# DRAM-to-DRAM copies in a selective scan: ScalarE's queue issues them in place of SyncE's

## The chip, the cores and the metric

One core of a Trainium2 chip. The metric is the device time of one execution in microseconds (us), lower is better. A core has TensorE (PE), VectorE (DVE), ScalarE (ACT), GpSimd (POOL) and SyncE (SP); SyncE computes nothing here and issues DMAs. ScalarE can issue DMAs too. Its DMA instructions stand in its one program, between its activations.

## The reference

The kernel computes a two-layer tower over 64 images of 37 tokens and 256 features: patch embedding, a selective scan, a mixture of experts, attention, a second mixture of experts. The change touches the scan alone, cut here to what matters:

```python
delta = softplus(x @ W_delta + b_delta)
Bm = x @ W_B + b_B
Cm = x @ W_C + b_C
A = -exp(A_log)
dA = exp(delta[..., None] * A)
dBx = delta[..., None] * Bm[:, :, None, :] * x[..., None]
def step(h, inputs):
    dA_t, dBx_t, C_t = inputs
    h = dA_t * h + dBx_t
    y_t = einsum('bdn,bn->bd', h, C_t)
    return (h, y_t)
```

The scan runs over L = 37 steps, one per token, for 64 images, 128 channels and 64 state columns.

## The kernel before

The program is written by hand: one function per engine, and semaphores between them. Nothing is scheduled by a planner, so the text of a function is its engine's order.

**A step of the scan.** The state of one step is a slab of 128 x 4096 numbers in SBUF, worked on in four groups (`GROUPS`), m = 0 to 3. For m = 0 and 2 TensorE multiplies B by delta times x into PSUM (`inject`, L1201), VectorE multiplies the old state by the decay (`decay_state`, L1999) and adds the two (`add_injected`, L2018). For m = 1 and 3 VectorE writes decay times state into PSUM (`seed_state`, L2007), TensorE adds the injection on top (`grow`, L1201) and ScalarE copies the result to SBUF (`copy_grown`, L1686). TensorE then reads the state out (`read_state`, L1234). Every second step ScalarE evicts the read-out (`evict_rows`, L1668), TensorE turns it (`turn_y`, L1245) and ScalarE copies it (`copy_y`, L1678).

**The decay factors** exp(delta * A) are made in blocks of four steps (`BLK`), one block ahead of their use: 32 "quads", each four matmuls of TensorE (`make_quad`, L1194) and one exponential of ScalarE (`exp_quad`, L1659), over three PSUM banks. `quads_made(t, m)` says which quads stand at which place: of step 1 of a block only m = 3 has some, its steps 2, 3 and 4 have them at every m. So the quads of block 1 stand from step 1, m = 3, to step 4, m = 3; those of block 2 from step 5, m = 3, to step 8, m = 3.

**The operands of step t** come from DRAM: SyncE loads them (`load_inject`, nine DMAs, L894 and L895) from `factor_rows`, three steps ahead at most (`INJ`), and each block's delta from `delta_rows` (`load_delta`, L880). Both tensors hold factors in three bf16 pieces, repeated over eight terms (`TERMS`). For the early steps (`RANGES[0]`) those rows are written straight from SBUF. For the later steps (`RANGES[1]`) the pieces are first kept once, in `late_rows` and `late_delta` (L846, L854), and then spread to eight terms by copies from DRAM to DRAM:
- `spread_delta` (L867): six copies, 3.6 MB, in `delta_rows`;
- `spread_rows` (L858): three copies for each of B and delta times x, each half of the partitions and each of two ranges of steps, 24 in all.

**Order on SyncE.** After the stores to `late_rows` its loop over t runs `load_inject(t)`, then at t = 3 `spread_delta`, at t = 4 a wait for it and `load_delta(2)`, at t = 4 to 7 and 9 to 12 one `spread_rows`. `load_inject(8)` and `load_inject(22)` wait for the copies they read. **On ScalarE** the first exponential of block 1 (step 1, m = 3) waits for the stores to `late_rows` and `late_delta`, since it overwrites their source in SBUF.

Of the kernel before, what the change touches and what calls it, by code (L numbers as in the profile page):

```python
# [12 lines left out]
P = 128  # L13
# [12 lines left out]
PAIRS = NI // 2  # L26
# [9 lines left out]
THALF = (L + 1) // 2  # L36
# [64 lines left out]
def build(nc, small, dense, patches, w_lin, a_rows, up0, dn0, w1, w2, b1, b2, gates_dram, slots,  # L101
          rows_dram, delta_dram, late_rows, late_delta, h_dram, gate_dram, out):
    with ExitStack() as ctx:
# [678 lines left out]
        def _(sp):  # L782
# [54 lines left out]
            def late_end(half, t1):  # L837

                return t1 - (1 if half and t1 == THALF else 0)
# [18 lines left out]
            def spread_rows(which, half, t0, t1):  # L858

                first = RANGES[1][2]  # L860
                n = late_end(half, t1)
                rows = late_rows[which, half, :, :, (t0 - first) * P:(n - first) * P]
                for k0, k1 in TOP_TERMS:
                    got = bc(rows[:, k0 // 3, :], 1, k1 - k0) if which else rows[:, 0:k1 - k0, :]
                    sp.dma_start(rows_dram[which, half, :, k0:k1, t0 * P:n * P], got).then_inc(factors_out, 16)

            def spread_delta():  # L867

                l0, l1, _, _ = RANGES[1]
                for i in range(2):  # L870
                    for k0, k1 in TOP_TERMS:
                        sp.dma_start(delta_dram[:, k0:k1, i, l0 * PAIRS:l1 * PAIRS],
                                     late_delta[:, 0:k1 - k0, i, :]).then_inc(delta_out, 16)

# [41 lines left out]
            for t in range(INJ, L):  # L916
# [5 lines left out]
                if t == 3:  # L922
                    sp.wait_ge(delta_out, 16 * 8)
                    spread_delta()
                if t == 4:
                    sp.wait_ge(delta_out, 16 * 14)
                    load_delta(2)
                    sp.wait_ge(factors_out, 16 * 16)
                if 4 <= t < 8:
                    spread_rows(1 - (t - 4) // 2, t % 2, 4, 11)  # L930
                if 9 <= t < 13:
                    spread_rows(1 - (t - 9) // 2, (t - 9) % 2, 11, THALF)
# [638 lines left out]
        def _(act):  # L1571
# [108 lines left out]

            def copy_grown(t, m):
# [13 lines left out]
            for t in range(L + 1):  # L1695
                for m in range(GROUPS):
                    if m == 1 and t % 2 == 1:
                        evict_rows(t // 2)
                    if t < L and m % 2 == 1:
                        copy_grown(t, m)  # L1700
                    if t < L and m == 3 and t % 2 == 1:
                        copy_y(t // 2)
                    for b, k in quads_made(t, m) if t < L else []:
                        if k == 0:
# [3 lines left out]
                            if b == 1:  # L1708
                                act.wait_ge(delta_out, 16 * 8)
                                act.wait_ge(factors_out, 16 * 16)  # L1710
# [683 lines left out]
```

## Time and profile before

| | us |
|---|---|
| median of 3 runs | 1105.67 (1104.58 to 1109.89) |
| the profiled execution, its own time | 1102.52 |
| its span | 1100.6 |
| TensorE busy | 925.5 (84%) |
| VectorE busy | 661.6 (60%) |
| ScalarE busy | 502.7 (46%) |
| mean granted TensorE clock | 0.923 |

The scan's steps lie between about 150 us and 460 us of the span. Rows of the profile name an engine, a line of the kernel, what is written and read, how often, and the idle time of the engine before, with what ended it. SPq and ACTq are the sequencers of SyncE and ScalarE: their rows are instructions that issue, wait or branch, not work of the engine.

### The profile page before, as it was taken

The numbers are of one execution on the slowest core, as the hardware profiler recorded it, in microseconds if no ns is written. First come the engines' busy times: TensorE is split into PE (matmuls) and PEld (weight loads), VectorE is DVE, ScalarE is ACT, GpSimd is POOL, SyncE is SP. The second block draws the span as 40 slices with busy tenths as digits, with TensorE's granted clock in tenths as the row PEclk, the third lists the DMA queues.
The fourth block names the chain that finished last, engine by engine and source line by source line (L and its number), as shares of the span: only waits on it lengthen the run. The fifth ranks groups of instructions, "written<-read, shape, count | busy, mean of one in ns | idle before, by whom it ended". The sixth has DMA issues, their size and how long they took to land.

```text
span 1100.6 us, 17569 instructions
## 1 busy us (share of the span) xinstructions
PE 925.5 (84%) x5861; PEld 583.1 (53%) x5862; DVE 661.6 (60%) x1172; ACT 502.7 (46%) x1019; POOL 308.6 (28%) x361
## 2 busy tenths in 40 slices
PE   8997497777777777699899999999999996459996
PEld 6773443333233332256677777657676764236664
DVE  2533966888889888864454445467777773213332
ACT  1226566777897777333222222334444432223332
POOL 4922782333323320000000000064345410512222
PEclk9998758988998889999999999989999996679999
DMA  6281767563212211861411111000000002322220
GB/s 245 96 293 77 225 172 242 157 175 79 52 34 55 49 30 32 325 249 59 136 45 45 44 44 44 0 1 1 1 1 0 1 1 106 152 90 92 82 84 26
DMA packets 96578, 100.30 MB, mean 91 GB/s; under 512 B 64638, under 2 KB 82815, under 8 KB 94848
## 3 DMA queue, kind: packets, MB, share of 16 engines
q1 hardware_dynamic: 93776, 92.14, 26.8%
q0 software_dynamic: 2736, 7.30, 1.8%
q8 instruction: 39, 0.64, 0.2%
q14 instruction: 27, 0.22, 0.1%
HBM read 72.84 MB, written 38.82 MB: 101 GB/s over the span
## 4 chain that ended last, share of the span: by engine, by line
PE 64%; ACT 12%; DVE 11%; issue 7%; SPq 2%; DMA 2%; POOL 1%; another core or an unknown queue 0%; ACTq 0%; DVEq 0%; POOLq 0%
PE ps L556 9%; PE ps L618 8%; PE ps L1234 6%; ACT mem L1659 5%; PE ps L1115 4%; PE ps L1518 4%; PE ps L1534 4%; PE ps L1431 3%; PE ps L1365 3%; PE ps L1194 3%; PE ps L1387 2%; PE ps L1201 2%; ACT mem L1686 2%; DVE mem L1999 2%; DVE mem L2018 2%
## 5 line engine op out<-in xcount | busy, mean ns | idle before, releaser
L1072 POOL TENSOR_TENSOR mem<-mem,sm 128x296 f32<-128x296 f32 x128 | 87.0, 714 | 346.1 <-ACT mem L1751 306.0
L1659 ACT ACTIVATE mem<-ps 128x512 f32<-128x512 f32 x288 | 154.0, 637 | 26.8 <-PE ps L1194 13.1
L1050 POOL TENSOR_SCALAR mem<-mem,sm 128x16 f32<-128x16 f32 x148 | 108.4, 754 | 153.8 <-PE ps L1234 153.8
L1194 PE MATMUL ps<-mem 64*128 64x128 bf16 x1140 | 92.9, 232 | 22.7 <-ACT mem L1659 13.6
L556 PE MATMUL ps<-mem 128*128 (+1 forms) x384 | 110.2, 416 | 0.6 <-DVE mem L529 0.6
L1234 PE MATMUL ps<-mem 128*32 128x512 f32 x592 | 90.2, 683 | 21.6 <-issue 12.8
L1686 ACT ACTIVATE mem<-ps 128x512 f32<-128x512 f32 x148 | 82.5, 610 | 55.1 <-PE ps L1201 54.9
L1194 PEld LDWEIGHTS ps<-mem 64*128 64x128 bf16 x1140 | 56.8, 100 | 92.2 <-ACT mem L1659 71.7
L2007 DVE TENSOR_TENSOR ps<-mem 128x512 f32<-128x512 f32 x144 | 93.6, 695 | 19.6 <-ACT mem L1686 19.1
L1201 PE MATMUL ps<-mem 64*128 64x512 bf16 x296 | 77.4, 430 | 32.8 <-DVE ps L2007 21.6
L1999 DVE TENSOR_TENSOR mem<-mem 128x1024 f32<-128x1024 f32 x72 | 88.0, 1223 | 25.0 <-ACT mem L1659 25.0
L618 PE MATMUL ps<-mem 128*128 128x296 f32 x352 | 99.9, 413 | 2.3 <-DVE mem L682 2.3
L642 ACT ACTIVATE mem<-ps 128x296 f32<-128x296 f32 x88 | 36.7, 417 | 135.0 <-PE ps L556 135.0
L2018 DVE TENSOR_TENSOR mem<-mem,ps 128x1024 f32<-128x1024 f32 x72 | 87.4, 1215 | 3.1 <-PE ps L1201 2.5
L556 PEld LDWEIGHTS ps<-mem 128*128 128x128 f32 x384 | 73.1, 191 | 25.1 <-issue 1.9
L618 PEld LDWEIGHTS ps<-mem 128*128 128x128 f32 x352 | 66.5, 190 | 24.1 <-DVE mem L682 3.7
L682 DVE TENSOR_TENSOR mem<-mem 128x296 f32<-128x296 f32 x88 | 41.1, 467 | 36.5 <-ACT mem L642 34.3
L1201 PEld LDWEIGHTS ps<-mem 64*128 64x128 bf16 x296 | 21.2, 97 | 73.9 <-DVE ps L2007 52.2
L1518 PE MATMUL ps<-mem 128*128 x104 | 51.1, 615 | 7.6 <-issue 7.1
L676 DVE TENSOR_TENSOR mem<-mem 128x296 f32<-128x296 f32 x64 | 29.9, 467 | 45.1 <-ACT mem L642 39.4
L1115 PE MATMUL ps<-mem 128*128 128x288 f32 x192 | 51.3, 421 | 5.0 <-DMA mem<-in_patches 5.0
L1091 POOL DMA_INDIRECT out_h<-mem,slot_token x26 | 25.6, 984 | 102.9 <-DVE mem L2277 99.3
(236 smaller groups left out, 1576.3 us busy)
## 6 DMA issues: line engine op xcount, KB each, us to landing
mem<-gates SPq DMA_DIRECT2D x7, 1184.0 KB, 6.1
mem<-in_w SPq DMA_DIRECT2D x2, 4096.0 KB, 16.2
slots<-mem SPq DMA_DIRECT2D x1, 6682.0 KB, 23.9
mem<-slots SPq DMA_DIRECT2D x26, 257.0 KB, 2.6
mem<-in_patches SPq DMA_DIRECT2D x7, 864.0 KB, 4.6
mem<-factor_rows SPq DMA_DIRECT2D x296, 16.0 KB, 1.7
mem<-factor_rows SPq DMA_DIRECT2D x37, 128.0 KB, 2.3
mem<-delta_rows SPq DMA_DIRECT2D x9, 512.0 KB, 4.6
```

What stands on the lines that cost most here:

```text
L556: mm = nc.tensor.matmul(ps[:, bank, 0:CH], w[:, k, row0:row0 + P], xn[:, k, cols], start=(k == 0), stop=(k == HALVES - 1))
L618: mm = nc.tensor.matmul(ps[:, 1 + 2 * cj + m, 0:CH], dn_w[:, j - 2, m * P:(m + 1) * P], hid2[:, b, :], start=(j == 2 and n == nt), stop=(j ...
L1050: nc.gpsimd.tensor_scalar(c_win4[:, t % SLOTS * 2 + r, :, w0:w0 + 8].rearrange("p j (x i) -> p j x i", i=2)[:, :, :, i], c_all[:, r * 16:r ...
L1115: mm = nc.tensor.matmul(ps[:, 2 * j + m, 0:IC * NP], wl[:, f, m * P:(m + 1) * P], xin[:, j, f, :], start=(f == 0), stop=(f == FK - 1))
L1194: mm = nc.tensor.matmul(ps[:, ring_bank(at_), e * BT:(e + 1) * BT], a_stat[64 * r:64 * r + 64, g, e, :], delta_in[b % 2][64 * r:64 * r + 6 ...
L1201: return nc.tensor.matmul(ps[:, bank, :], b_in[t % INJ][rows, m, :], dx_in[t % INJ][rows, m, :, :].rearrange("p x n -> p (x n)"), start=st ...
L1234: mm = nc.tensor.matmul(ps[32 * j:32 * j + 32, Y_BANK, :], c_win[:, win:win + 32], slot[slot_of(t)][:, quad * 512:(quad + 1) * 512], start ...
L1518: mm = nc.tensor.matmul(ps[:, 2 + j, 0:HID1], slot_xT[j][:, k, :], w1s[:, k, ds(e * HID1, HID1)], start=(k == 0), stop=(k == 1))
L1659: nc.scalar.activation(decay_slots[b % 2][:, :, 4 * k:4 * k + 4], ps[:, ring_bank(at_), :].rearrange("p (e t) -> p t e", e=4), ACT.Exp).th ...
L1686: nc.scalar.activation(slot[slot_of(t)][:, quad * 512:(quad + 1) * 512], ps[:, GROW_BANK + half, :], ACT.Copy).then_inc(copied, 1)
L1999: nc.vector.tensor_tensor(now[:, gs], now[:, gs], before[:, gs], ALU.mult).then_inc(multed, 1)
L2018: nc.vector.tensor_tensor(now, now, ps[:, INJ_BANK:INJ_BANK + 2, :], ALU.add).then_inc(added, 1)
```

## The change

`spread_rows` and `spread_delta` move from SyncE's function to ScalarE's, with `act.dma_start` for `sp.dma_start`. `spread_delta` stands before the wait for the `late_rows` stores at step 1, m = 3. `spread_rows` stands at m = 0 of steps 2 to 5 and 9 to 12. SyncE keeps the wait ahead of `load_delta(2)` and loses one for `late_rows`. The bytes and the copies are the same.

```diff
@@ SyncE
-            def spread_rows(which, half, t0, t1):
-            def spread_delta():
...
                 load_inject(t)
-                if t == 3:
-                    sp.wait_ge(delta_out, 16 * 8)
-                    spread_delta()
                 if t == 4:
                     sp.wait_ge(delta_out, 16 * 14)
                     load_delta(2)
-                    sp.wait_ge(factors_out, 16 * 16)
-                if 4 <= t < 8:
-                    spread_rows(1 - (t - 4) // 2, t % 2, 4, 11)
-                if 9 <= t < 13:
-                    spread_rows(1 - (t - 9) // 2, (t - 9) % 2, 11, THALF)
@@ ScalarE
+            def spread_rows(which, half, t0, t1):
+
+                first = RANGES[1][2]
+                n = t1 - (1 if half and t1 == THALF else 0)
+                rows = late_rows[which, half, :, :, (t0 - first) * P:(n - first) * P]
+                for k0, k1 in TOP_TERMS:
+                    got = bc(rows[:, k0 // 3, :], 1, k1 - k0) if which else rows[:, 0:k1 - k0, :]
+                    act.dma_start(rows_dram[which, half, :, k0:k1, t0 * P:n * P], got).then_inc(factors_out, 16)
+
+            def spread_delta():
+
+                l0, l1, _, _ = RANGES[1]
+                for i in range(2):
+                    for k0, k1 in TOP_TERMS:
+                        act.dma_start(delta_dram[:, k0:k1, i, l0 * PAIRS:l1 * PAIRS],
+                                     late_delta[:, 0:k1 - k0, i, :]).then_inc(delta_out, 16)
...
                     if m == 1 and t % 2 == 1:
                         evict_rows(t // 2)
+                    if m == 0 and 2 <= t < 6:
+                        spread_rows(1 - (t - 2) // 2, t % 2, 4, 11)
+                    if m == 0 and t == 9:
+                        act.wait_ge(factors_out, 16 * 28)
+                    if m == 0 and 9 <= t < 13:
+                        spread_rows(1 - (t - 9) // 2, (t - 9) % 2, 11, THALF)
                     if t < L and m % 2 == 1:
                         copy_grown(t, m)
...
                             if b == 1:
                                 act.wait_ge(delta_out, 16 * 8)
+                                spread_delta()
                                 act.wait_ge(factors_out, 16 * 16)
```

ScalarE's program, from the copy of the first read-out (step 1, m = 3) to the eviction of step 3. Before (L1659 the exponentials, L1686 `copy_grown`):

```order
L1678 ACTIVATE mem<-ps 128x64 [waits b_split,made]
L1659 ACTIVATE mem<-ps 128x128x4 [waits delta_out,factors_out,seeded,made,multed,read_ps]
L1659 ACTIVATE mem<-ps 128x128x4 [waits made] x3
L1686 ACTIVATE mem<-ps 128x512 [waits grown] x2
L1659 ACTIVATE mem<-ps 128x128x4 [waits made] x5
L1686 ACTIVATE mem<-ps 128x512 [waits grown] x2
L1659 ACTIVATE mem<-ps 128x128x4 [waits made] x5
L1668 ACTIVATE mem<-ps 128x512 [waits read_ps]
```

Now, at the same place (the exponentials are L1634, `copy_grown` L1678, the eviction L1643):

```order
L1670 DMA delta_rows<-late_delta 128x3x896 x2
L1670 DMA delta_rows<-late_delta 128x2x896
L1634 ACTIVATE mem<-ps 128x128x4 x2
L1663 DMA factor_rows<-late_rows 64x3x896 x2
L1663 DMA factor_rows<-late_rows 64x2x896
L1634 ACTIVATE mem<-ps 128x128x4 x2
L1678 ACTIVATE mem<-ps 128x512 x2
L1634 ACTIVATE mem<-ps 128x128x4 x5
L1678 ACTIVATE mem<-ps 128x512 x2
L1634 ACTIVATE mem<-ps 128x128x4 x3
L1663 DMA factor_rows<-late_rows 64x3x896 x2
L1663 DMA factor_rows<-late_rows 64x2x896
```

The first two rows come twice (six DMAs) ahead of the exponential that waits for `late_rows`; a group of three stands between the second and third exponential of step 2's place, and after the third of five at step 3's.

SyncE's program after the `late_rows` stores, before (L894 and L895 are the nine loads of a step, steps 3 and 4 here):

```order
L894 DMA mem<-factor_rows 16x4x128 x8
L895 DMA mem<-factor_rows 128x4x128
L872 DMA delta_rows<-late_delta 128x3x896 x2
L872 DMA delta_rows<-late_delta 128x2x896
L872 DMA delta_rows<-late_delta 128x3x896 x2
L872 DMA delta_rows<-late_delta 128x2x896
L894 DMA mem<-factor_rows 16x4x128 x8
L895 DMA mem<-factor_rows 128x4x128
L880 DMA mem<-delta_rows 128x16x128
```

Now (L877 and L878 are the loads, L863 is `load_delta`):

```order
L877 DMA mem<-factor_rows 16x4x128 x8
L878 DMA mem<-factor_rows 128x4x128
L877 DMA mem<-factor_rows 16x4x128 x8
L878 DMA mem<-factor_rows 128x4x128
L863 DMA mem<-delta_rows 128x16x128
```

Step 4's loads follow step 3's with nothing between.

## Rows read from the trace of the kernel before

**Rows 1.** The page: the chain that ended last, shares of the span by engine.
```profile
PE 64%; ACT 12%; DVE 11%; issue 7%; SPq 2%; DMA 2%; POOL 1%; another core or an unknown queue 0%; ACTq 0%; DVEq 0%; POOLq 0%
```

**Rows 2.** Waits, 100 to 200 us: who waited for whom, total, times, longest.
```profile
ACT mem L1659 <- DMA late_rows<-mem: 4.9, 1, 4.9
...
PE ps L1201 <- DMA mem<-factor_rows: 1.9, 2, 1.6
```

**Rows 3.** Waits, 200 to 440 us.
```profile
PEld ps L1194 <- ACT mem L1659: 59.3, 112, 0.9
```

**Rows 4.** Timeline of SyncE's queue: start us, us, what, times.
```profile
153.77 7.69 SPq L846 DMA_DIRECT2D late_rows<-mem  x4
161.57 8.51 SPq L894 DMA_DIRECT2D mem<-factor_rows  x8
...
170.59 4.31 SPq L872 DMA_DIRECT2D delta_rows<-late_delta  x6
175.01 5.06 SPq L894 DMA_DIRECT2D mem<-factor_rows  x8
...
185.87 2.39 SPq L865 DMA_DIRECT2D factor_rows<-late_rows  x3
...
199.45 1.83 SPq L865 DMA_DIRECT2D factor_rows<-late_rows  x3
201.38 3.81 SPq L894 DMA_DIRECT2D mem<-factor_rows  x8
```

**Rows 5.** The chain in order of time, at step 4's load.
```profile
180.11 6.91 DMA mem<-factor_rows
```

**Rows 6.** Timeline of ScalarE, steps 2, 4 and 8; in brackets idle time before.
```profile
169.41 2.07 ACT L1659 ACTIVATE mem<-ps 128x512 f32<-128x512 f32 x4 [4.91 <-DMA late_rows<-mem]
...
189.90 1.08 ACT L1659 ACTIVATE mem<-ps 128x512 f32<-128x512 f32 x2 [3.46 <-PE ps L1194]
...
222.61 1.08 ACT L1659 ACTIVATE mem<-ps 128x512 f32<-128x512 f32 x2 [0.59 <-PE ps L1194]
```

**Rows 7.** Stretches: engines' busy time, then clock, DMA share and GB/s.
```profile
166.00:168.00 2.00, 0.05 (x1) 0.00 (x0) 1.12 (x1) 0.00 (x0) 2.00 (x4) 1.00 0.80 270
168.00:170.00 2.00, 0.00 (x0) 0.00 (x0) 0.00 (x0) 0.59 (x2) 0.17 (x1) 1.00 0.25 61
```

**Rows 8.** ScalarE's sequencer (ACTq: last numbers, first and last start) and activations, 78 to 82 us.
```profile
L432 ACTq EVENT_SEMAPHORE  x1: 17/17/17, 79.7 to 79.7; - x1
...
L473 ACTq ALU_OP  x1: 35/35/35, 81.0 to 81.0; - x1
...
79.95 0.50 ACT L1590 ACTIVATE mem<-ps,sm 128x296 f32 x1
...
80.97 0.45 ACT L436 ACTIVATE mem<-mem 128x296 f32<-128x296 f32 x1
```

**Rows 9.** The same at steps 5 and 9.
```profile
L1667 ACTq EVENT_SEMAPHORE  x1: 17/17/17, 195.1 to 195.1; - x1
...
195.41 1.61 ACT L1659 ACTIVATE mem<-ps 128x512 f32<-128x512 f32 x3
...
199.38 1.21 ACT L1686 ACTIVATE mem<-ps 128x512 f32<-128x512 f32 x2 [1.86 <-PE ps L1201]
...
232.26 1.26 ACT L1686 ACTIVATE mem<-ps 128x512 f32<-128x512 f32 x2 [2.03 <-PE ps L1201]
```

**Rows 10.** Timeline of TensorE's decay products (L1194) at steps 7 and 8.
```profile
211.90 0.27 PE L1194 MATMUL ps<-mem 64*128 64x128 bf16 x2
...
213.80 0.41 PE L1194 MATMUL ps<-mem 64*128 64x128 bf16 x8
...
220.77 0.27 PE L1194 MATMUL ps<-mem 64*128 64x128 bf16 x2
```

**Rows 11.** Timeline of ScalarE at step 10.
```profile
238.95 1.09 ACT L1659 ACTIVATE mem<-ps 128x512 f32<-128x512 f32 x2 [0.18 <-PE ps L1194]
240.42 1.08 ACT L1659 ACTIVATE mem<-ps 128x512 f32<-128x512 f32 x2 [0.38 <-PE ps L1194]
```

More of the change, by code:

```diff
@@ L856, in keep_late_delta @@
                                  ).then_inc(delta_out, 16)
-            def spread_rows(which, half, t0, t1):
[L860 to L865, printed above, removed]
-            def spread_delta():
[L869 to L873, printed above, removed]
             def load_delta(b):
```

## The prediction

> **What bounds the kernel now.** I read the page first. The table above has TensorE busy for 84% of the span and ScalarE for 46%; the chain of work that ended last is 64% TensorE and 12% ScalarE [rows 1]. Those are averages. The change touches one stage only, the scan, and in it only steps 1 to 12, some 164 us to 265 us of the span. After step 12 both programs issue the same instructions.
>
> Next the table of waits. Before 200 us it has two waits for a DMA that the change can move: ScalarE's exponentials waited 4.9 us for the `late_rows` stores, and TensorE's injections waited 1.9 us, in two pieces, for a load from `factor_rows` [rows 2]. From 200 us to 440 us no wait for a DMA stands in that table; its long repeated entry is TensorE's weight loads waiting for ScalarE's exponentials, 59.3 us over 112 times [rows 3]. So ScalarE is the engine that paces the scan while a block of decay factors is being made, and SyncE's queue costs something at one or two places only.
>
> The timeline of SyncE shows why [rows 4]. Its queue issues four `late_rows` stores in 7.69 us, then step 3's nine loads, then the six copies of `spread_delta` (4.31 us), and only then step 4's nine loads, from 175.01 on. The last of these is issued at 180.11 and lands 6.91 us later, at 187.02, in the chain in order of time [rows 5]. ScalarE felt that as 3.46 us of idle time before its exponentials at 189.90 [rows 6]. At step 8, which has the same place in its block and no DMA to wait for, the same idle time is 0.59 us [rows 6]. **The load of step 4 therefore costs 3.46 - 0.59 = 2.9 us**, and 2.9 us is all that freeing SyncE's queue can give: no later step waits for SyncE.
>
> **The change part by part.** 30 DMA instructions (6 of `spread_delta`, 24 of `spread_rows`, same bytes, same number) leave SyncE and stand in ScalarE's program.
>
> *SyncE.* Step 4's loads follow step 3's directly. They start near 170.6 instead of 175.0, and no longer lie behind the six copies in one first-in, first-out queue, though they share the DMA engines with them. TensorE began to wait for them 1.6 us [rows 2] before 187.02, at about 185.4. With 5.06 us for eight of them [rows 4] the last would be issued near 176, and have some nine us to land. The second piece of that wait, 0.3 us at step 5, falls where ScalarE is busy without a gap, and is no term. Term: **-2.9 us**.
>
> *`spread_delta` on ScalarE.* The exponentials' wait of 4.91 us, from about 164.5 to 169.41 [rows 6], is where these six instructions go. Issued at SyncE's pace they take 4.31 us [rows 4], so they end near 168.6, inside the wait: cost 0. If that cover is gone, 0.8 us is all that is left of it. Upper end: the `late_rows` stores needed 7.69 / 4 = 1.92 us each while the rings were full [rows 4]; six of those are 11.5 us, 6.6 us past the wait. I take 4.31, the row of the very same copies.
>
> But the copies now run beside the stores that ScalarE waits for. The DMA share is 0.80 from 166 to 168 us and 0.25 in the two us after [rows 7]. The copies' first packets would come some 2 us after 164.3, when the tail of the stores is left and engines begin to go idle. Lower end 0. Upper end: the 270 GB/s of 166 to 168 us [rows 7] are 0.54 MB, and if each packet of them alternates with one of a copy, their 2 us double: 2 us. Taken: **+1.0 us**. The Trainium skill ("DMA: Bandwidth & Descriptors", Queues, rings and completion order) says that each DMA engine goes round the queues that have work, a packet at a time. By that rule the stores are slowed, and it speaks against the change here, where one queue served them first. No row of this trace has two hardware queues at work.
>
> *The 24 copies of `spread_rows` on ScalarE.* They stand in eight groups of three. A group took SyncE 2.39 us beside other traffic and 1.83 without [rows 4]; I use 1.85. What it costs ScalarE depends on how far its sequencer runs ahead of its datapath. Two rows say how. The `EVENT_SEMAPHORE` of L432 ran at 79.7, before the activation of L1590, which stands ahead of it in the program, began at 79.95; and L473's `ALU_OP`, which waits for nothing, ran at 81.0, when the activation ahead of it (L436, 80.97) had what it waited for, the end of the one before [rows 8]. So the sequencer does not wait for the datapath, but stops at an instruction whose semaphore has not come. How deep it runs is seen at step 5: L1667 ran at 195.1 with three exponentials not yet begun (195.41 and on) [rows 9]. That is the very place where step 5's group is put.
>
> Place by place, with a group beginning when the exponential ahead of it has its semaphore:
> - Steps 5 and 9: 195.1 + 1.85 = 196.95, about where the three exponentials end (195.41 + 1.61), and after the eviction that follows them ScalarE sat idle 1.86 us and 2.03 us anyway [rows 9]. Cost 0.
> - Steps 3 and 11, read from step 7: TensorE's third decay product of the step ended near 212.1, its next ones at 214.2 [rows 10]. 212.2 + 1.85 = 214.05. Cost 0.
> - Steps 4 and 12, from step 8: third product at 221.0 [rows 10], 221.05 + 1.85 = 222.9 against the next exponential at 222.61 [rows 6]: 0.3 each.
> - Step 10: the pair at 238.95 lets the group start; 240.8 against 240.42 [rows 11]: 0.4.
> - Step 2: all four exponentials from 169.41 on ran without a gap, 2.07 us in all, so one per 0.5 us [rows 6]. The group starts at 169.45 and ends at 171.3, where the third began near 170.4: 0.9.
>
> Together **+1.9 us**, all at places where ScalarE paces the scan. Lower end 0. Upper end: nothing is hidden, six groups by 1.85 are 11.1 us, and the slack of steps 5 and 9 is overrun by about 0.5 each: +12.1.
>
> **Sum:** -2.9 + 1.0 + 1.9 = 0.0 us. The profiled execution took 1102.52 us (span 1100.6), 3.15 us under the median of the runs, 1105.67, which itself lies in a spread of 1104.58 to 1109.89. The sum moves either by nothing, so I forecast the median: **1105.7 us**, no change.
>
> **The rivals.**
>
> *A. A DMA on ScalarE waits until the datapath is empty, or holds it.* (The other side.) The rows on the sequencer show semaphore and register instructions, no DMA. If a DMA instruction lets nothing be in flight, each of the six groups in a paced stretch costs its full 1.85 us and steps 5 and 9 some 0.5 us each. 12.1 + 1.0 - 2.9 = +10.2: **1115.9 us**. It decides from the point at which more than half of a group is exposed, since six halves are 5.6 us. For: where ScalarE paces the scan nothing absorbs it. Against: L1667 and L432 [rows 8, 9]. Chance 0.17.
>
> *B. The two queues take turns in making descriptors.* SyncE issues nine loads in each step, eight of them in 3.81 us, so one every 0.47 us [rows 4]. If ScalarE's instruction has to wait for one load each time it meets them, a group is 3 x 0.3 = 0.9 us longer on average. Step 3's eight loads took 8.51 us in place of 3.81 while data was backed up [rows 4]; beside them `spread_delta` would end near 171 rather than 168.6: 1.6 us past the wait. Six groups by 0.9 minus 0.2 us of slack, plus 1.6, give +6 at most, and half of it if the two seldom meet: +3, **1108.7 us**. For: those 8.51 us. Chance 0.17. The Trainium skill ("Perfetto Trace Analysis", Per-engine timelines) describes the generator of descriptors as locked for one user at a time. No run before has two users.
>
> *C. The sequencer runs past waiting activations too.* Then every group is hidden behind the queue, the 1.9 us vanish, and the result is 1.0 - 2.9 = -1.9: **1103.8 us**. Against: L473 at 81.0 [rows 8]. Chance 0.08. The Trainium skill ("Perfetto Trace Analysis", Per-engine timelines) has this one: the wait is held in a queue beside the sequencer, which is ready for the next instruction as soon as it has pushed. The trace disagrees, by that row.
>
> *D. Step 4's load is late all the same*, because it alternates with 3.6 MB of copies. Nothing comes of the -2.9: **1108.6 us**. Against: nine us between its issue and its use. Chance 0.08.
>
> **How the numbers follow.** The forecast, within 1.5 us of 1105.7, has the remaining 0.50. Half a per cent is 5.5 us, about what a measurement of this kernel can tell from no change. A gain over that is out of reach of every case, as 2.9 us is all there is: 0.03, for what I do not see. Slower by more: A with its 0.17, and 0.04 from B's upper end: 0.21. The rest, 0.76, is no change. The range: C and the lower ends of the forecast reach down to 1102.5 (-2.9 and nothing paid); upward B and D and the first part of A, up to 1114, which leaves out the fuller half of A, some 0.1, and little below.
>
> **What would show it.** Right: ScalarE's wait for `late_rows` ends 0 to 2 us later than 169.41; no wait for `factor_rows` at step 4; 30 DMA issues on ScalarE, some of them starting before exponentials that precede them in the program; gaps before the next exponential of about 0.9 us at step 2, 0.3 to 0.4 us at steps 4, 10 and 12, none at 3, 5, 9 and 11. A shows as gaps of 1.9 us in each of six groups; B as issues of over 0.8 us on ScalarE; D as the old wait at step 4. The forecast is wrong if the time from 164 us to the end of step 12 differs by over 2 us from before, and anything from step 13 on that differs is not of this argument.

## The result and the profile after

Over 20 executions of each, the changed kernel took 1111.93 us in the median (1105.28 to 1117.08) and the kernel before 1104.99 (1097.59 to 1110.46). The ratio is 1.0066, 95% interval 1.0049 to 1.0083: slower, by 7.3 us (5.4 to 9.2; the ratio times 1105). The forecast was 1105.7 and no change. The result lies inside the stated range (1102.5 to 1114), but above the half per cent that divided "no change" from "slower".

| | before | after |
|---|---|---|
| span of the profiled execution, us | 1100.6 | 1110.1 |
| mean granted TensorE clock | 0.923 | 0.912 |
| TensorE, VectorE, ScalarE busy, us | 925.5, 661.6, 502.7 | 932.2, 662.9, 502.9 |

The page of the changed kernel: its DMA queues (packets, MB, share of 16 engines), then the chain that ended last.

```profile
q1 hardware_dynamic: 87152, 80.86, 23.5%
q10 hardware_dynamic: 6624, 11.27, 3.1%
...
PE 65%; ACT 13%; DVE 9%; issue 7%; DMA 3%; ACTq 2%; another core or an unknown queue 1%; SPq 0%; POOL 0%; DVEq 0%; POOLq 0%
```

q10 is ScalarE's queue, which had no work before. In the chain SPq has gone from 2% [rows 1] to 0%, and ACTq from 0% to 2%: the path that ran through SyncE's queue now runs through ScalarE's.

The waits of the changed kernel, 160 to 200 us and then 200 to 440 us, answer [rows 2, 3].

```profile
ACT mem L1634 <- DMA delta_rows<-late_delta: 6.6, 1, 6.6
```
```profile
PEld ps L1169 <- ACT mem L1634: 60.4, 112, 1.0
```

The two `factor_rows` waits are gone, and ScalarE's exponential waits 6.6 us in place of 4.9. The label names `delta_rows` data, but the timeline of ScalarE says otherwise. It answers [rows 6, 9, 11]; ACTq rows are its sequencer's, and the number in brackets is idle time of the engine before the row.

```profile
163.93 6.69 ACTq L1670 DMA_DIRECT2D delta_rows<-late_delta  x6
170.72 0.60 ACT L1634 ACTIVATE mem<-ps 128x512 f32<-128x512 f32 x1 [6.65 <-DMA delta_rows<-late_delta]
170.76 1.10 ACTq L1663 DMA_DIRECT2D factor_rows<-late_rows  x1
171.21 0.59 ACT L1634 ACTIVATE mem<-ps 128x512 f32<-128x512 f32 x1
171.90 1.81 ACTq L1663 DMA_DIRECT2D factor_rows<-late_rows  x2
173.76 1.08 ACT L1634 ACTIVATE mem<-ps 128x512 f32<-128x512 f32 x2 [1.95 <-issue]
...
180.22 0.54 ACTq L1663 DMA_DIRECT2D factor_rows<-late_rows  x1
...
180.79 0.63 ACTq L1663 DMA_DIRECT2D factor_rows<-late_rows  x1
...
181.45 2.44 ACTq L1663 DMA_DIRECT2D factor_rows<-late_rows  x1
183.93 1.09 ACT L1634 ACTIVATE mem<-ps 128x512 f32<-128x512 f32 x2 [1.97 <-issue]
...
191.70 0.54 ACTq L1663 DMA_DIRECT2D factor_rows<-late_rows  x1
191.71 1.08 ACT L1634 ACTIVATE mem<-ps 128x512 f32<-128x512 f32 x2
192.27 1.27 ACTq L1663 DMA_DIRECT2D factor_rows<-late_rows  x2
193.59 1.09 ACT L1634 ACTIVATE mem<-ps 128x512 f32<-128x512 f32 x2 [0.81 <-PE ps L1169]
...
198.77 0.52 ACTq L1663 DMA_DIRECT2D factor_rows<-late_rows  x1
199.11 0.63 ACT L1634 ACTIVATE mem<-ps 128x512 f32<-128x512 f32 x1
199.32 0.62 ACTq L1663 DMA_DIRECT2D factor_rows<-late_rows  x1
```

Three readings. First, the exponential at 170.72 starts 0.1 us after the sixth issue ends (163.93 + 6.69 = 170.62): it waited for its own sequencer, which still stood at the DMAs. The six took 6.69 us and not the 4.31 of [rows 4]. Second, the groups of steps 2 and 3 have single DMAs of 1.10 and 2.44 us, and both leave idle time put down to "issue", 1.95 and 1.97 us; those of steps 4 and 5 take 0.5 to 0.64 us a DMA. Third, at step 5 the DMA at 198.77 stands in the program behind the exponential of 199.11 and ran before it.

The chain in order of time says the same of 163.93 to 170.7: nothing but the six issues.

```profile
163.93 0.61 ACTq L1670
164.57 1.80 ACTq L1670
166.39 1.26 ACTq L1670
167.68 0.67 ACTq L1670
168.38 1.17 ACTq L1670
169.57 1.04 ACTq L1670
```

SyncE's queue in the changed kernel, beside [rows 4]:

```profile
153.07 7.56 SPq L846 DMA_DIRECT2D late_rows<-mem  x4
160.74 10.14 SPq L877 DMA_DIRECT2D mem<-factor_rows  x8
...
171.56 4.30 SPq L877 DMA_DIRECT2D mem<-factor_rows  x8
```

Step 4's loads start at 171.56, 3.4 us sooner, as forecast; but step 3's take 10.14 us to issue where they took 8.51. The landing times in the traces say more. The last of step 3's loads lands at 179.2, 179.7 and 181.7 us in the three profiles of the changed kernel, against 172.5, 170.4 and 173.1 before. The last of step 4's lands at 185.3, 184.7 and 187.5, against 187.0, 184.9 and 187.5: issued sooner, it lands hardly sooner.

**Where the time went in the stretch.** I measured the time from ScalarE's first `copy_y` (step 1, m = 3; 164.21 in the first profile of before) to its first `copy_grown` of step 13, 101.25 us there, with the markers between. Two further profiles of each kernel are among the experiments. Differences against the first profile of before, us:

| piece | forecast | three profiles of after |
|---|---|---|
| to step 2, m = 1 (`spread_delta`, step 2's group) | +1.9 | +3.8, +2.8, +4.8 |
| to step 3, m = 3 (step 3's group) | 0 | +2.5, +1.5, +0.7 |
| to step 4, m = 1 (step 4's load and group) | -2.6 | -2.2, -2.3, -2.0 |
| to step 9, m = 3 | 0 | -0.2, -0.3, 0.0 |
| to step 13, m = 1 (groups of steps 10 to 12) | +0.7 | +1.2, +1.2, +1.3 |
| sum | 0.0 | +5.1, +2.9, +4.8 |

The other two profiles of before give -0.3 and +0.2 for the whole. So the stretch holds +4.3 us of the 7.3; the rest lies outside it. (The 7.3 is of 20 executions, the 4.3 of three profiles of each kernel.)

### The profile page after: what moved, and what is told of

The parts are those of the page before. It is cut to its first block, busy times and chain, and to the rows that moved or that the text cites. A ratio compares the mean times of both kernels' runs of the same rounds, so it can differ in the third digit from the quotient of the medians.

```text
span 1110.1 us, 17569 instructions
## 1 busy us (share of the span) xinstructions
PE 932.2 (84%) x5861; PEld 587.9 (53%) x5862; DVE 662.9 (60%) x1172; ACT 502.9 (45%) x1019; POOL 309.9 (28%) x361
## 4 chain that ended last, share of the span: by engine, by line
PE 65%; ACT 13%; DVE 9%; issue 7%; DMA 3%; ACTq 2%; another core or an unknown queue 1%; SPq 0%; POOL 0%; DVEq 0%; POOLq 0%
PE ps L556 8%; PE ps L618 8%; PE ps L1209 6%; ACT mem L1634 6%; PE ps L1493 4%; PE ps L1090 4%; PE ps L1509 4%; PE ps L1169 4%; PE ps L1406 3%; PE ps L1340 3%; ACT mem L1678 2%; PE ps L1176 2%; PE ps L1362 2%; DVE mem L1998 2%; PE ps L1220 2%
## 5 line engine op out<-in xcount | busy, mean ns | idle before, releaser
L1634 ACT ACTIVATE mem<-ps 128x512 f32<-128x512 f32 x288 | 154.1, 636 | 31.2 <-PE ps L1169 11.5
L1678 ACT ACTIVATE mem<-ps 128x512 f32<-128x512 f32 x148 | 82.3, 610 | 55.0 <-PE ps L1176 54.8
```

The costliest lines, as they stand in the source:

```text
L1634: nc.scalar.activation(decay_slots[b % 2][:, :, 4 * k:4 * k + 4], ps[:, ring_bank(at_), :].rearrange("p (e t) -> p t e", e=4), ACT.Exp).th ...
L1678: nc.scalar.activation(slot[slot_of(t)][:, quad * 512:(quad + 1) * 512], ps[:, GROW_BANK + half, :], ACT.Copy).then_inc(copied, 1)
```

## The experiments

In this table "stretch" is as above, against 101.25 us; "scan's end" is the time from the last `copy_grown` of the scan (step 36, m = 3) to ScalarE's next operation of the stage behind it (L426), 10.8 us in the first profile of before. The ratio is to runs of before on the same chip.

| kernel | stretch, us | scan's end, us | ratio, 95% interval |
|---|---|---|---|
| before, three profiles | 0, -0.3, +0.2 | 10.8, 11.8, 15.0 | |
| after, three profiles | +5.1, +2.9, +4.8 | 14.7, 14.7, 14.7 | 1.0066 (1.0049 to 1.0083) |
| late_only | +0.3 | 12.4 | 1.0014 (0.9990 to 1.0038) |
| delta_only | +3.4 | 10.8 | 1.0008 (0.9989 to 1.0027) |
| early_only | +5.4 | 14.7 | 1.0056 (1.0031 to 1.0081) |
| act_alone | +8.4 | 14.7 | 1.0094 (1.0063 to 1.0124) |
| later_groups | +2.4 | 14.7 | 1.0068 (1.0039 to 1.0098) |
| sp_reordered | -3.0 | 10.8 | 1.0004 (0.9974 to 1.0034) |
| sp_reordered_again | -2.9 | 10.8 | 1.0015 (0.9985 to 1.0045) |
| delayed | -0.5, then +3.7 | 10.8 | 1.0045 (1.0019 to 1.0071) |

### Both kernels again (again_before, again_after)

> The kernel before, profiled a second time, to see what one profile differs from another without any change. Measure: the stretch from ScalarE's first read-out copy (L1678, step 1) to its copy at step 13, m = 1 (L1686 after the eviction of step 13), 101.25 us in the first profile. If the stretch is the same within 0.5 us and the rest of the span moves by 2 to 4 us, the 4.5 us that the changed kernel loses outside the stretch are scatter of the clock. If the rest is the same within 1 us, they belong to the change.

> The changed kernel, profiled a second time. Its stretch was 106.31 us. Both theories expect the stretch again within 0.5 us. Outside it the first profile lost 4.5 us against before, 3 of them at the end of the scan, where TensorE ran at half its clock; if that is scatter, it will not be there in full again.

One execution each: before 1097.98 us (span 1096.1), after 1113.88 (span 1112.0). The stretch repeats to within 0.3 us for before, but only 2.2 us for after, where I expected 0.5. Outside the stretch before moved by 4.2 us, and after lost the same 3.9 us at the scan's end again. One term of the prediction does not repeat so well in before itself: the piece from step 3, m = 3, to step 4, m = 1, in which step 4's load is waited for, took 7.16 us in the first profile and 5.19 in this one, while the piece ahead of it took 0.7 us longer. Without the wait it takes 4.29 us (sp_reordered_again, below), so the wait cost 0.9 us here, 1.6 with what the piece ahead lost, and 2.9 and 2.8 us in the first and third profiles. The piece behind it was 0.9 us longer here too; TensorE waited 1.3 us there for step 5's load (0.3 in the first profile). What step 4's load costs is 0.9 to 2.9 us from profile to profile, not a firm 2.9.

### One part alone: the late groups (late_only)

The 12 copies of steps 9 to 12 go to ScalarE; all else stays.

```diff
-                if 9 <= t < 13:
-                    spread_rows(1 - (t - 9) // 2, (t - 9) % 2, 11, THALF)
@@ ScalarE
+                    if m == 0 and t == 9:
+                        act.wait_ge(factors_out, 16 * 28)
+                    if m == 0 and 9 <= t < 13:
+                        spread_rows(1 - (t - 9) // 2, (t - 9) % 2, 11, THALF)
```

> Only the 12 copies of steps 9 to 12 are issued by ScalarE; spread_delta and the copies of steps 4 to 7 stay on SyncE. Theory T (ScalarE loses only what sticks out behind the exponentials that its sequencer ran ahead of; in a quiet stretch little): steps 9 to 13 cost 1.1 us more, as in the changed kernel, ratio 1.001. Rival H (a DMA on ScalarE holds the datapath): 3 x 1.85 + 0.5 = 6 us, ratio 1.0055.

Measured 1107.0 us. Between step 9, m = 3, and step 13 the stretch grows by 1.0 us: 0.6 at step 10, 0.4 at step 12, none at step 11. The timeline of ScalarE at step 10:

```profile
239.48 0.54 ACTq L1686 DMA_DIRECT2D factor_rows<-late_rows  x1
239.93 0.59 ACT L1657 ACTIVATE mem<-ps 128x512 f32<-128x512 f32 x1
240.05 1.30 ACTq L1686 DMA_DIRECT2D factor_rows<-late_rows  x2
241.39 1.08 ACT L1657 ACTIVATE mem<-ps 128x512 f32<-128x512 f32 x2 [0.87 <-PE ps L1192]
```

0.87 us of idle time where before had 0.38 [rows 11]. The 0.4 at step 12 is firm: that step took 7.89 us in all three profiles of before. Step 10 alone took 8.45 to 9.00 us in them and 9.15 here, so 0.15 to 0.7 us of it is the copies'. The forecast for these groups, 0.4 and 0.3, was of the right size. The rival of 6 us, that a DMA holds the datapath, is refuted. The ratio cannot tell 1 us from nothing.

### One part alone: the six copies of delta (delta_only)

```diff
-                if t == 3:
-                    sp.wait_ge(delta_out, 16 * 8)
-                    spread_delta()
@@ ScalarE
                                 act.wait_ge(delta_out, 16 * 8)
+                                spread_delta()
                                 act.wait_ge(factors_out, 16 * 16)
```

> Only spread_delta is issued by ScalarE, all 24 copies of spread_rows by SyncE. Theory T: the six issues take 6.7 us again and end 1.7 us later than the old wait did; step 4's load comes in time, which gives back 2.9 us; together -1.2 us, ratio 0.999. Rival D' (the gain at step 4 comes only because steps 2 and 3 are already late in the changed kernel): the load is late again and nothing is given back, +1.7 us, ratio 1.0015.

Measured 1106.85 us, no difference that can be told (0.9 us, -1.2 to +3.0), though the stretch of its profile is 3.4 us longer. Neither -1.2 nor +1.7, my two expectations, is what the stretch shows. Its waits, 160 to 200 us:

```profile
ACT mem L1656 <- DMA delta_rows<-late_delta: 6.6, 1, 6.6
...
PEld ps L1198 <- DMA mem<-factor_rows: 2.8, 1, 2.8
...
PE ps L1198 <- DMA mem<-factor_rows: 2.7, 1, 2.7
```

Two things. The wait at the start is 1.7 us longer than 4.9 with no group behind it: that is the price of `spread_delta` on ScalarE. (In the eight profiles with those copies on SyncE this wait is 4.1 to 5.4 us, in the six with them on ScalarE 6.0 to 7.5, so the price is about 2 us.) And TensorE waits 2.7 us for a load again, one step earlier: the piece with step 3 grew by 3.6 us and that with step 4 shrank by 2.9. The wait for step 4's load was removed and one for step 3's took its place.

### The other part alone: the early groups (early_only)

The four groups of steps 2 to 5 go to ScalarE; `spread_delta` and the late groups stay on SyncE.

```diff
                     load_delta(2)
-                    sp.wait_ge(factors_out, 16 * 16)
-                if 4 <= t < 8:
-                    spread_rows(1 - (t - 4) // 2, t % 2, 4, 11)
@@ ScalarE
+                    if m == 0 and 2 <= t < 6:
+                        spread_rows(1 - (t - 2) // 2, t % 2, 4, 11)
```

> One part of the change alone: the four groups of spread_rows for the first range of steps stand on ScalarE at steps 2 to 5, as in the change; spread_delta and the late groups stay on SyncE. The theory (what was lost early is copies issued while the DMA engines are full of other traffic): at steps 2 and 3 the groups meet step 3's loads and spread_delta, which both stand on SyncE, so they should cost at least as much as in the change, 2.1 and 1.9 us, and step 4's load is still behind spread_delta (wait of 2 to 3 us, or more as three more copies go before it); step 9 to 12 nothing. Stretch to the end of step 12: +3 to +6 us. The rival (it was spread_delta on ScalarE that did the harm, the groups cost 0.9 and 0 there): +1 to +2 us. In both, wherever the scan's end shows a half-clock piece of some 14 us as in the change, 3.9 us on top.

Measured 1110.15 us, slower by 0.56%. SyncE's timeline and TensorE's at step 4:

```profile
163.62 9.01 SPq L894 DMA_DIRECT2D mem<-factor_rows  x8
...
173.33 6.32 SPq L872 DMA_DIRECT2D delta_rows<-late_delta  x6
179.76 6.68 SPq L894 DMA_DIRECT2D mem<-factor_rows  x8
```
```profile
194.49 0.60 PE L1198 MATMUL ps<-mem 64*128 64x512 bf16 x2 [4.80 <-DMA mem<-factor_rows]
```

The six copies take 6.32 us to issue on SyncE too, with copies of another queue under way. So the 6.69 us are not a property of ScalarE. The step-2 group costs 0.9 us and step 3's 0.7 here, about the forecast at step 2 and 0.7 over it at step 3; the large loss, 3.4 us, is at step 4, whose load still stands behind `spread_delta`, which itself takes longer, and now shares the DMA engines with groups: it lands at 194.4. My expectation that steps 2 and 3 would cost as much as in the change was wrong: in the change they have `spread_delta` directly ahead of them in the same queue, here they don't.

### ScalarE's copies without SyncE's loads beside them (act_alone)

The change, but SyncE waits for the stores before step 3's loads.

```diff
             for t in range(INJ, L):
+                if t == 3:
+                    sp.wait_ge(factors_out, 16 * 16)
                 load_inject(t)
```

> The changed kernel with one wait more: SyncE waits for the late_rows stores before it issues step 3's loads, so that ScalarE issues the six copies of spread_delta with no load of SyncE's beside them. If the two sequencers share one generator of descriptors and SyncE's loads blocked it, the six issues take 4.3 to 4.9 us in place of 6.7 and ScalarE goes on 1.4 us earlier. If the copies themselves were held up behind the stores' data (full DMA engines), they take 6.7 us again.

Measured 1112.66 us. All instances of `spread_delta` (duration in ns, min, median, max; then first and last start):

```profile
L1672 ACTq DMA_DIRECT2D delta_rows<-late_delta x6: 607/1038/1745, 164.8 to 170.1; - x6
```

The six still take 6.47 us. SyncE issued nothing from 161.6 until 169.83; by then five had been started, and those five took 5.3 us (5.6 in the changed kernel), where before all six took 4.31. Two queues taking turns at making descriptors (rival B) can't be the reason. What is left is the data already under way, the stores' and the copies' own; that the issue waits for it is argued from this, not seen in a row. That TensorE then waits 3.9 us for step 3's load is this experiment's own cost.

### The early groups where ScalarE has slack (later_groups)

The change, with the groups of steps 2 to 5 at steps 4 and 5.

```diff
-                    if m == 0 and 2 <= t < 6:
-                        spread_rows(1 - (t - 2) // 2, t % 2, 4, 11)
+                    for g in {(4, 0): (0,), (5, 0): (1,), (5, 2): (2, 3)}.get((t, m), ()):
+                        spread_rows(1 - g // 2, g % 2, 4, 11)
```

> The changed kernel with the four early groups of spread_rows elsewhere: one at step 4, m = 0, one at step 5, m = 0, two at step 5, m = 2, where ScalarE sat idle 1.9 and 3.1 us. Theory T: the 2.1 us at step 2 and the 2.5 us at step 3 go, the gain at step 4 stays, some 0.7 us at step 4 and 0.6 us at step 5 are paid: stretch 102 to 103 us, ratio about 1.001 to 1.002. Rival H (a DMA holds the datapath wherever it stands): the same 12 issues of 0.6 us cost the same, stretch 106.

Measured 1110.86 us, no better than the change, where 1.001 to 1.002 was expected. The stretch is 103.65 us, nearer to theory T (102 to 103) than to 106. In the stretch the pieces to step 2, m = 1, and to step 3, m = 3, are +2.1 and +0.3 against a mean of +3.8 and +1.6 for the change: the groups of steps 2 and 3 cost 1.7 and 1.3 us there. What is left of the first piece, 2.1 us, is `spread_delta`, as in delta_only (1.7). By the stretch this kernel should be 1.8 us faster than the change; the ratio doesn't show it, and doesn't exclude it.

### SyncE alone, with step 4's loads ahead of the copies (sp_reordered, sp_reordered_again)

Before, with `spread_delta` moved behind step 4's loads; nothing on ScalarE.

```diff
-                if t == 3:
-                    sp.wait_ge(delta_out, 16 * 8)
-                    spread_delta()
                 if t == 4:
-                    sp.wait_ge(delta_out, 16 * 14)
-                    load_delta(2)
+                    sp.wait_ge(delta_out, 16 * 8)
+                    spread_delta()
                     sp.wait_ge(factors_out, 16 * 16)
+                if t == 5:
+                    sp.wait_ge(delta_out, 16 * 14)
+                    load_delta(2)
```

> Nothing on ScalarE: SyncE issues step 4's loads first and spread_delta after them, load_delta(2) after step 5's loads. Theory T: the 2.9 us at step 4 are had for nothing, stretch 98.4 us against 101.25, ratio 0.9975. If step 4's load was not what held the scan (rival: TensorE would have waited for something else there), the stretch stays at 101.25.

> The reordered kernel (all copies on SyncE, spread_delta behind step 4's loads) once more, since its first comparison could not tell: its profile had the stretch of steps 1 to 12 2.96 us shorter than before, and the part ahead of the stretch, which is the same program, 3.3 us longer. If the gain is real it shows again in the stretch, -2.3 to -3.0 us against the profiles of before, with ScalarE's wait at step 4 under 1 us, and the total is -2 to -3 us, a ratio near 0.9975. If the first stretch was chance, the stretch is within 1 us of before. If the gain is given back elsewhere by something that the order causes, the stretch is shorter and the ratio again 1.000 or above.

The stretch is 3.0 and 2.9 us shorter, and ScalarE's gap at step 4 is the 0.59 us of step 8 [rows 6] in both; the rows are of the second profile:

```profile
177.30 4.17 SPq L872 DMA_DIRECT2D delta_rows<-late_delta  x6
```
```profile
188.35 1.09 ACT L1659 ACTIVATE mem<-ps 128x512 f32<-128x512 f32 x2 [0.59 <-PE ps L1194]
```

So the wait at step 4 is real and can be removed without ScalarE; step 4's last load lands at 180.0 and 179.2. But the 3.0 and 2.9 us are not all of that kind. The piece at step 4 is 2.9 us shorter in both. The piece to step 2, the same program as before, is 0.8 and 0.7 us shorter, since the stores were waited for 4.1 and 4.2 us and not 4.9. And the piece to step 9 is 0.6 and 0.7 us longer, since step 5's load now stands behind the copies, and TensorE waits for it (160 to 200 us, second profile; 2.4 us in the first):

```profile
PE ps L1201 <- DMA mem<-factor_rows: 2.7, 1, 2.7
```

What the order gives is therefore 2.2 us against the first profile of before, and less against one in which the load costs less. The total doesn't show even that: the two comparisons gave 1105.31 and 1105.91 us, ratios of 1.0004 and 1.0015; the second interval excludes the ratio near 0.9975 that I expected. In both profiles the part ahead of the stretch was 3.3 and 2.1 us longer than in the first profile of before; it is the same program there, and over all fourteen profiles its length varies between -1.5 and +3.3 us. Whether the order causes that is open, and I can't call this version faster.

### A pure delay (delayed), and both kernels a third time

Before, with the first exponential of block 4 (step 13) run seven more times; the output stays the same.

```diff
+                for n in range(7 if b == 4 and k == 0 else 0):
+                    nc.scalar.activation(decay_slots[b % 2][:, :, 4 * k:4 * k + 4],
+                                         ps[:, ring_bank(at_), :].rearrange("p (e t) -> p t e", e=4),
+                                         ACT.Exp).then_inc(again, 1)
+                    act.wait_ge(again, n + 1)
```

> Before, with one pure delay: the first exponential of block 4 (step 13) is run seven more times, each waiting for the last, some 4.5 us on ScalarE, with every DMA where it was. The output is unchanged. Four traces of kernels with all copies on ScalarE had a piece of 13.7 us at half the TensorE clock at the scan's end, 3.9 us long in cost, which before lacks. Theory 1: the clock there depends on how the time until then falls, and a delay of this size brings it too: the time from the last copy_grown of the scan to the second exponential behind it is 3.9 us longer, total +7 to +8 us. Theory 2: it belongs to the DMA traffic or the copies' place and not to the time: no such piece, total +3 to +4.5 us.

> The kernel before once more, for its profile: does the scan's end run at full clock (as in one profile of two, the other had 3.4 us at half clock)? If the half-clock piece there belongs to the change, none of 13.7 us here; if it is chance, in about half of the profiles.

> The changed kernel once more: if the half-clock piece at the scan's end belongs to it, 13.7 us again, with 3.9 us of cost; the stretch of steps 1 to 12 between +2.9 and +5.1 us against the first profile of before, as in its two earlier ones.

These look for what is outside the stretch. In the change a slow piece comes at the scan's end. Stretches of 2 us of the first profile of before (busy time and count for PE, PEld, DVE, ACT, POOL; granted clock, DMA share, GB/s), then of the changed kernel, then of the third profile of before:

```profile
464.00:466.00 2.00, 1.94 (x8) 1.14 (x7) 1.97 (x6) 0.00 (x0) 0.00 (x0) 1.00 0.98 418
...
468.00:470.00 2.00, 2.00 (x10) 1.53 (x9) 1.64 (x4) 0.32 (x1) 0.00 (x0) 1.00 0.83 356
```
```profile
464.00:466.00 2.00, 1.45 (x7) 1.45 (x8) 0.00 (x0) 0.50 (x1) 0.00 (x0) 0.50 0.55 129
...
468.00:470.00 2.00, 1.60 (x3) 1.18 (x4) 1.04 (x3) 0.00 (x0) 0.00 (x0) 0.50 1.00 424
```
```profile
464.00:466.00 2.00, 1.09 (x2) 0.84 (x3) 1.52 (x4) 0.00 (x0) 0.00 (x0) 0.50 1.02 436
...
468.00:470.00 2.00, 2.00 (x6) 1.37 (x5) 1.89 (x5) 0.00 (x0) 0.00 (x0) 0.50 1.24 533
```

At half the clock (the 1.2 GHz level) the same eight matmuls of the next stage take twice as long, before and after:

```profile
462.44 2.23 PE L1290 MATMUL ps<-mem 128*128 128x296 f32 x8 [1.77 <-DVE mem L2038]
```
```profile
468.40 4.29 PE L1265 MATMUL ps<-mem 128*128 128x296 f32 x8 [1.77 <-DVE mem L2037]
```

The piece costs 3.9 us (14.7 - 10.8). It stands in all three profiles of the change and in the three experiments that have the change's early groups or all of it on ScalarE (early_only, act_alone, later_groups): six of six. But it also stands in the third profile of before (15.0 us), in part in again_before and late_only, and in none of delta_only, delayed and the two of sp_reordered. So it does not belong to the change alone. The profile of the pure delay does not have it: a scan's end of 10.8 us. But that profile is of one of the quickest of its 12 executions, 1104.68 us (1104.58 to 1113.13), and before has the piece in one profile of three, so one profile without it says little. The total is 1108.32 us, 4.8 us over before (interval 2.1 to 7.8), of which 3.7 us are the delay itself; that fits theory 2 better than the 7 to 8 us of theory 1, whose lower end it doesn't exclude.

The granted clock of all executions on record adds to this. Its mean is lower than that of the runs of before on the same chip by 0.003, 0.007 and 0.004 in early_only, act_alone and later_groups, by 0.001 in late_only, delta_only and both of sp_reordered, and by 0.002 in delayed. In the 20 executions of the change it is 0.907, where before had 0.913 to 0.915 in the comparisons of the experiments. 13.7 us at half clock in place of full (so long is the piece in all three profiles of the change) lower the mean by 13.7 x 0.5 / 1105 = 0.006. So a lower clock goes with the early groups on ScalarE over many executions, and by about the size of this piece; nothing on record tells why.

## Why the prediction was right in its range and wrong in its terms

**The range.** That 1111.9 us lies between 1102.5 and 1114 is luck as far as the mechanism goes. The range reached so high for A, B and D, and none of them, as described, is what made the kernel slower. (Its lower end should have been 1105.7 - 2.9 = 1102.8.) By the prediction's own sign, a stretch that differs by over 2 us, the forecast was wrong.

**Right.** The sequencer's behaviour, on which the forecast chose between its rivals. DMAs on ScalarE ran ahead of exponentials that precede them (198.77 before 199.11) and while ScalarE was busy, so A is refuted. A's sign, gaps of 1.9 us, stands at steps 2 and 3 alone (1.95 and 1.97), where the issues themselves are long; those at steps 4, 10 and 12 are 0.81, 0.87 and 1.16 us, 0.2 to 0.6 over before's.

They did not run past an exponential whose semaphore had not come, so C is refuted. Step 2's group can't show it, as the sequencer was at the six copies until 170.62. Step 4's can. It stands in the program behind three exponentials (191.22 and the two from 191.71 on), the last of which waits for this product of TensorE:

```profile
191.38 0.27 PE L1169 MATMUL ps<-mem 64*128 64x128 bf16 x2
```

It ended at 191.65, and the group started at 191.70, with only the first of the three exponentials begun. At step 5 it had started with three not yet begun, so room behind the sequencer was not what held it. The Trainium skill ("Perfetto Trace Analysis", Per-engine timelines), which has the sequencer ready for the next instruction once it has pushed the waiting one, is contradicted by this trace at that place.

B is refuted by act_alone, and by step 4: three issues took 1.84 us (191.70 to 193.54) while SyncE issued eight loads in 3.97 us, about what each takes alone (1.83 and 3.81 [rows 4]). Its sign, issues of over 0.8 us on ScalarE, did appear (1.1 to 2.4 us), but it appeared in act_alone too and so did not tell B from data under way.

```profile
190.80 3.97 SPq L877 DMA_DIRECT2D mem<-factor_rows  x8
```

D's sign, the old wait at step 4, is gone: no wait for `factor_rows` over 0.3 us is left in any profile of the change. But its mechanism is there. Step 4's load lands only 0.0 to 1.7 us sooner than before, and is in time because step 4 itself comes some 4 us later.

The places and sizes of the quiet groups were right within about half a us: 0 at steps 5, 9 and 11, and +1.2 in sum from step 9 to step 13 for the forecast +0.7.

**Wrong: the term "`spread_delta` on ScalarE", cost 0 + 1.0.** The step that failed is "Issued at SyncE's pace they take 4.31 us". That row was of nearly idle DMA engines: their share just before it was 0.25 [rows 7]. At the new place the stores' data was still under way, and the six took 6.69 us, and 6.08 to 7.54 us in the other five profiles with them on ScalarE. It is 1.7 us more than the wait they were to hide in (delta_only), and the issue, not the stores' landing (168.97), ended the wait. The prediction had a row of a crowded system as its upper end (the stores' 1.92 us each) and took the other; at 1.1 us each the truth lies between. The extra microsecond for stores slowed by copies is not seen: their landing took 9.6 us in the median, 9.9 before. So the term of +1.0 came out of the wrong reason and was about 1 us too small.

**Wrong: "The 24 copies", +1.9.** It held for the quiet ones. Step 2's group was put at 0.9 and costs 1.7, step 3's at 0 and costs about 1.3 (against later_groups). The prediction used 1.85 us for both, while 3.6 MB of copies are being written; step 2's took 2.95 us (170.76 to 173.71), and one DMA of step 3's took 2.44. What was moved then points to why. DMA by queue, 170 to 174 us, before and then after:

```profile
q1 hardware_dynamic: 944, 0.62, 59.2%
```
```profile
q10 hardware_dynamic: 842, 1.44, 96.6%
q1 hardware_dynamic: 339, 0.07, 8.7%
```

The copies hold 97% of sixteen engines' time, and what SyncE's queue moves beside them, the small packets of the loads, is 339 packets, though SyncE issued eight more loads from 171.56 on. Step 3's loads land 7 to 9 us later than before. The Trainium skill ("DMA: Bandwidth & Descriptors", Queues, rings and completion order) has each engine go round its queues a packet at a time; in these rows a copy's packet is some 1.7 KB (1.44 MB over 842) and a load's some 0.2 KB, so by that rule, if one of these packets is one turn, a load that shares the engines waits for a copy's packet at each of its own. The trace agrees in direction; no row shows the turns themselves.

**Half right: "-2.9 us".** The piece at step 4 gave -2.2, -2.3 and -2.0 with step 4's group in it. But the same traffic now runs beside step 3's loads, and in delta_only and act_alone TensorE waits 2.7 and 3.9 us for those, in later_groups 0.6. In the change this wait is covered because ScalarE is late anyway, so what the loads lose and what ScalarE loses do not add: removing the second exposes part of the first.

**Not foreseen: what is outside the stretch.** 7.3 - 4.3 = 3 us. The clock at the scan's end is the likeliest part of it: 3.9 us in three of three profiles of the change, and 0, 1.1 and 4.2 in those of before, a mean difference of 2.2 us, and the granted clock of all executions points the same way. It is not shown by a run that switches it, and what decides that clock is open. The part behind the scan's end, the same program in both, took 633.4, 630.7 and 635.1 us in the profiles of before and 634.9, 638.4 and 634.7 in those of the change; it moves by 4.4 us within before alone, so profiles can't say whether it takes part. The totals minus the stretch for the other kernels run from -2.5 (delta_only) to +5.1 us (later_groups), so no experiment here resolves the last 3 us.

The summary of it: the terms sum to 0.0 by the prediction and to +4.3 by the traces, because three durations (the six copies and the groups of steps 2 and 3) were taken from rows of a quiet DMA system and used in a crowded one. Where the remaining 3 us of the total went stays open.

## What to carry to other kernels

What a DMA issue costs the engine that issues it depends on the data under way. Price it from a row with the same traffic beside it, not from the same instruction elsewhere: here 0.5 to 0.6 us became 1.1 to 2.4 on ScalarE at the moment that mattered. An engine that computes and is paced (ScalarE here) is the wrong place for issues that can be held up; to get a load out from behind a bulk copy, move the copy behind the load in the same queue first. Here that removed the wait at step 4, 2.9 us, and brought one for step 5's load that gave 0.6 back, and no gain in the total could be told. And a second queue takes away the protection that order in one queue gave: with the copies beside them, step 3's small loads landed 7 to 9 us later.

## What was unexpected about the hardware

- Six issues of DRAM-to-DRAM copies took 4.17 to 4.46 us on SyncE with little else under way (seven profiles), 6.32 us on SyncE and 6.1 to 7.5 us on ScalarE with other data under way. The cost goes with the traffic and not with the engine that issues.
- A wait that the profile puts down to DMA data was one for the engine's own sequencer: the exponential began 0.1 us after the last issue. Where the "wait" ends with a row of ACTq, read that row.
- The part ahead of the stretch, the same program in all kernels, differs by up to 4.7 us between profiles. The stretch repeated to 0.5 us in the three profiles of before, so that a change of 2 or 3 us can be read there (in the changed kernel it repeats to 2.2 us only), and was lost in the totals of 12 executions.
- The granted clock at one place (the scan's end) was half or full from execution to execution of one kernel, worth 3.9 us.
